# Four tiles of 32 array columns in place of two of 64 for the softmax denominators

## What is computed

```python
h = _layernorm(x, axis=-1) * (1 + ca) + sa
# attention, 8 heads of 64; keys and values come from one latent of 64 columns
q = (h @ Wq.T).reshape(b, t, 8, 64)
kv_latent = h @ Wkv_down.T
k = (kv_latent @ Wk_up.T).reshape(b, t, 8, 64)
v = (kv_latent @ Wv_up.T).reshape(b, t, 8, 64)
scores = jnp.einsum('bqhd,bkhd->bhqk', q, k) * scale
attn = jax.nn.softmax(scores, axis=-1)          # the denominators belong to this
out = jnp.einsum('bhqk,bkhd->bqhd', attn, v)
x = x + ga * (out.reshape(b, t, 512) @ Wo.T)
h = _layernorm(x, axis=-1) * (1 + cb) + sb
x = x + gb * (h @ weight.T + pooled(h) @ disha)
```

## Time and profile before

| | us |
|---|---|
| median of three runs | 3296.38 |
| the profiled execution | 3298.7 |
| its span, first to last instruction | 3296.9 |
| PE busy | 3215.7 (98%) |
| POOL busy | 2569.9 (78%) |
| DVE busy | 2218.1 (67%) |
| ACT busy | 1730.9 (53%) |
| 4096 records of L545 (mixes), busy together | 991.9 |
| 512 records of L631 (denominators), busy together | 133.1 |

### The profile page before, as it was taken

The page is one execution under the profiler, slowest core; times in us unless marked ns, Lnnn a source line. Parts: engine busy times, 40 slices in busy tenths (PEclk is TensorE's granted clock), DMA queues, the critical chain, the costliest instruction groups (busy, mean ns, idle before and its releaser), DMA issues.

```text
span 3296.9 us, 43601 instructions
## 1 busy us (share of the span) xinstructions
PE 3215.7 (98%) x14886; PEld 1944.6 (59%) x14886; DVE 2218.1 (67%) x2542; ACT 1730.9 (53%) x3203; POOL 2569.9 (78%) x1513
## 2 busy tenths in 40 slices
PE   5999999999999999999999999999999999999995
PEld 3555656566566565656566565665666666566554
DVE  4657667776767768667776767768667776766652
ACT  1555555555555555555555555555555555555551
POOL 1778788887887878788887877878788887877882
PEclk7999999999999999999999999999999999999996
DMA  2111120111112011111111112011121111111111
GB/s 67 39 45 53 46 65 33 52 56 46 55 46 65 30 59 52 46 65 33 52 55 46 55 46 65 31 58 52 46 65 33 52 55 46 55 46 52 37 40 35
DMA packets 157644, 163.06 MB, mean 49 GB/s; under 512 B 54384, under 2 KB 105712, under 8 KB 157424
## 3 DMA queue, kind: packets, MB, share of 16 engines
q1 hardware_dynamic: 157424, 160.29, 14.9%
HBM read 74.66 MB, written 17.33 MB: 28 GB/s over the span
## 4 chain that ended last, share of the span: by engine, by line
PE 92%; DVE 5%; POOL 1%; issue 1%; ACT 1%; DMA 1%; SPq 0%; POOLq 0%; ACTq 0%; DVEq 0%
PE ps_mix L545 27%; PE ps_score L563 16%; PE ps_max L584 14%; PE ps_score L565 14%; PE ps_side L533 6%; PE ps_side L644 6%; PE ps_side L631 3%; PE ps_side L662 3%; DVE neg_max L982 1%; DVE w_out_lo L991 1%; PE ps_side L602 1%; POOL prob_sum L840 1%; DVE query L1025 1%; PE ps_side L651 1%; DVE h_lo L1015 1%
## 5 line engine op out<-in xcount | busy, mean ns | idle before, releaser
L840 POOL TENSOR_TENSOR prob_sum<-prob_sum,probs 128x1024 f32<-128x1024 f32 x768 | 1880.9, 2449 | 283.4 <-ACT probs L720 239.3
L982 DVE TENSOR_REDUCE neg_max<-ps_max 128x1 f32<-128x1024 f32 x1024 | 1247.6, 1220 | 776.4 <-PE ps_max L584 769.8
L720 ACT ACTIVATE probs<-ps_score 128x512 f32<-128x512 f32 x2048 | 1114.4, 599 | 945.5 <-PE ps_score L565 921.0
L545 PE MATMUL ps_mix<-probs,values 128*64 128x512 f32 x4096 | 991.9, 605 | 0.0
L563 PE MATMUL ps_score<-query,key_hi 128*128 128x512 f32 x2048 | 874.1, 427 | 1.1 <-ACT probs L720 1.1
L565 PE MATMUL ps_score<-query_m,key_lo 128*128 128x512 f32 x2048 | 807.2, 394 | 0.0
L584 PE MATMUL ps_max<-key_hi,query 128*128 128x512 f32 x2048 | 644.2, 396 | 8.0 <-DVE neg_max L982 5.2
L563 PEld LDWEIGHTS ps_score<-query,key_hi 128*128 128x128 f32 x2048 | 385.6, 188 | 377.1 <-issue 296.9
L545 PEld LDWEIGHTS ps_mix<-probs,values 128*64 128x64 f32 x4096 | 248.7, 136 | 477.3 <-issue 476.5
L840 POOL TENSOR_TENSOR prob_sum<-probs 128x1024 f32<-128x1024 f32 x128 | 320.8, 2507 | 241.1 <-ACT probs L720 241.1
L584 PEld LDWEIGHTS ps_max<-key_hi,query 128*128 128x128 f32 x2048 | 386.9, 190 | 100.9 <-DVE neg_max L982 10.5
(11 more groups left out here) (119 smaller groups left out, 2983.4 us busy)
## 6 DMA issues: line engine op xcount, KB each, us to landing
query_m<-query SPq DMA_DIRECT2D x128, 512.0 KB, 3.2
recip<-recip_scratch SPq DMA_DIRECT2D x256, 128.0 KB, 2.9
x_in<-in_L_attn_x_dram SPq DMA_DIRECT2D x32, 512.0 KB, 4.0
x_mid<-in_L_attn_x_dram SPq DMA_DIRECT2D x64, 256.0 KB, 4.3
out_dram<-x_mid SPq DMA_DIRECT2D x64, 256.0 KB, 2.2
denoms<-recip SPq DMA_DIRECT2D x256, 2.0 KB, 1.8
gates<-gates_scratch SPq DMA_DIRECT2D x16, 256.0 KB, 4.1
query_m<-max_row SPq DMA_DIRECT2D x128, 4.0 KB
```

The source lines that it names most:

```text
L545: last = nc.tensor.matmul(ps_mix[j * R:j * R + R, :], values[par][:, k, :], probs[:, s % RING, j * HALF:(j + 1) * HALF], start=(k == 0), s ...
L720: nc.scalar.activation(probs[:, s % RING, half * HALF:(half + 1) * HALF], ps_score[half], ACT.Exp, scale=SCALE).then_inc(exps_done, 1)
L840: nc.gpsimd.tensor_tensor(out=total[:, :], in0=before, in1=probs[:, s % RING, :], op=ALU.add).then_inc(adds_done, 1)
L982: nc.vector.tensor_reduce(neg_max[:, m:m + 1], ps_max[m % 2][:, :], AX_X, ALU.max, negate=True).then_inc(maxima_done, 1)
```

## The change

The sum over the partitions is taken by four matmuls instead of two. Each has 32 result rows (not 64) and goes over 256 of the 1024 columns (not 512). The result rows q*32 to q*32+31 of `ps_side` then hold the sums of quarter q in columns 0 to 255. The copy by ScalarE is 128 by 256 instead of 128 by 512. The spread to `denoms` takes four DMAs of 32 partitions instead of two of 64, with the same 1024 numbers, and VectorE's wait counts 64 instead of 32 per denominator. Nothing else is touched: the order on every engine is the same, with two more matmuls and two more DMA issues in the places of the old ones.

```diff
+QUARTERS = 4
+QR, QC = P // QUARTERS, T // QUARTERS
 # SP
-for j in range(2):
-    sp.dma_start(denoms[j * R:(j + 1) * R, :], prob_total[j * R:j * R + 1, :]).then_inc(denoms_spread, 16)
+for q in range(QUARTERS):
+    sp.dma_start(denoms[q * QR:(q + 1) * QR, :], prob_total[q * QR:q * QR + 1, 0:QC]).then_inc(denoms_spread, 16)
 # TensorE
-for j in range(2):
-    last = nc.tensor.matmul(side[j * R:(j + 1) * R, :], ones_cols[:, :],
-                            prob_sum[i % 2][:, j * HALF:(j + 1) * HALF], start=True, stop=True)
+for q in range(QUARTERS):
+    last = nc.tensor.matmul(side[q * QR:(q + 1) * QR, 0:QC], ones_cols[:, 0:QR],
+                            prob_sum[i % 2][:, q * QC:(q + 1) * QC], start=True, stop=True)
 # ScalarE
-nc.scalar.activation(prob_total[:, :], ps_side[:, :], ACT.Copy).then_inc(side_drained, 1)
+nc.scalar.activation(prob_total[:, 0:QC], ps_side[:, 0:QC], ACT.Copy).then_inc(side_drained, 1)
 # VectorE
-need(dve, denoms_spread, 32 * (GROUPS * b + i + 1))
+need(dve, denoms_spread, 16 * QUARTERS * (GROUPS * b + i + 1))
```

## The result

The changed kernel took 3261.5 us (median of four runs, 3258.6 to 3262.6), the kernel before 3298.7 (four runs, 3295.1 to 3303.5): a ratio of 0.9889, 95% interval 0.9875 to 0.9904. It is faster by 37 us, 1.1%. Profile against profile the executions took 3262.6 and 3298.7 us, the spans 3260.8 and 3296.9: 36.1 us less either way.

The account below looks back on a forecast made before the run. TensorE's queue, 98% busy, was taken as the bound. Gains of 27.7 and 9.5 us, 37.2 together, less 1.0 and 0.9 gave 35.3: profiled 3298.7 to 3263.4, median forecast 3261 us, range 3247 to 3284.

Parts of the forecast that it names:

- The bound and the share on the path: TensorE's queue bounds the run; denominators hold 3.5% of the chain, 115 us; shorter pieces give 37.2 us.
- The piece behind the mixes: 99 denominators directly behind the mixes on TensorE: 0.86 us each becomes 0.58, 27.7 us gained.
- rivals 1 and 2: Denominator records: 1, only two run at once, 3311 us, chance 0.10; 2, four slow each other, near 3286, chance 0.09.
- The entry: TensorE's switch from 64-column to 32-column tiles before a denominator: 0.13 us taken, bounds 0 and 0.20.
- the rule quoted in the prediction: Trainium skill, array packing: changing the tiling mode drains TensorE, unlike changing the tile; without it 13 us more gained.
- rival 3: The switch into 32-column tiles is hidden altogether: 0.45 us in place of 0.58 for the 99, 3248 us, chance 0.06.
- The piece that waited: 27 denominators that began after a wait on TensorE: 1.08 us each becomes 0.73, 9.5 us gained.
- These waits stay as they are: TensorE's waits ending at denominators keep their length, since VectorE's query, ending the longer, is fed by TensorE and comes earlier.
- ScalarE's copy and SP's issues: Copy 384 ns instead of 598; four DMA issues some 2.3 us instead of 1.14; VectorE keeps 1.5 us of cover.
- rival 4: Slower spread makes VectorE wait for reciprocals and TensorE in part: 32 us given back, about 3293 us, chance 0.05.
- The end: End of the run: 1 us off where POOL is nearly full, 0.9 us lost on the last copy and spread.

Follow-up runs that it names:

- narrow512: Kernel before with only the tile width changed: four tiles of 32 array columns, each still over 512 data columns; 3308.7 us, ratio 1.0033 to the kernel before.
- half64: Kernel before, still two tiles of 64 array columns, each matmul over only the first 256 columns of its half; 3245.7 us, ratio 0.9840.
- thin_add: Changed kernel with two of GpSimd's 56 adds per slot cut to 8 columns and one added to every sum; 3250.9 us, ratio 0.9864 to the kernel before.
- mix4_after: Changed kernel with VectorE's multiplication by the reciprocals one step earlier (MIX_LAG 4 for 5); 3255.8 us, ratio 0.9872 to the kernel before.
- copy512: Changed kernel with ScalarE's copy over all 512 columns as before; 3265.3 us, ratio 0.9894 to the kernel before.
- one_dma: Changed kernel with the spread as one DMA in place of four; 3260.7 us, ratio 0.9885 to the kernel before.
- pair_grouped: Changed kernel's 32-column, 256-data-column matmuls on two tiles only, program order quarters 0, 1, 2, 3; 3311.5 us, ratio 1.0034 to the kernel before.
- pair_turns: Changed kernel's 32-column, 256-data-column matmuls on two tiles only, program order quarters 0, 2, 1, 3; 3305.6 us, ratio 1.0021 to the kernel before.

## Why the prediction was right

The forecast was 3261, the median is 3261.5; the range and the side were right. So close a hit is luck in part: I took 35.3 us off a median of 3296.4; with its fourth run the kernel before has a median of 3298.7, and from there it fell by 37.2. By its steps:

- **The bound and the share on the path.** As said: TensorE is the queue, and the pieces carry the gain. 98 x 0.29 + 27 x 0.44 = 40.3 us on the pieces, where I had 37.2.
- **The piece behind the mixes.** 0.58 forecast, 0.57 measured. Four tiles work together at full rate (rivals 1 and 2 fell; narrow512 and the two pair kernels show that neither the narrow tile nor the short stream makes the gain without it). Against the 3.07 times that the Trainium skill gives for four tiles in rows ("TensorE: Matmul & The Clock Gate", Measured speedup vs the span model), eight records of 0.216, 1.73 us, took 0.45 here behind the entry, 3.8 times.
- **The entry.** 0.13 taken, 0.12 measured, 0.10 of it ahead of the first record; half64, which lacks it, has 0.43 for 0.57. So a change of tiling mode costs something, as the rule quoted in the prediction wants it, and rival 3 fell. That TensorE drains in it no run shows.
- **The piece that waited.** This term was mis-sized: 0.73 forecast, 0.64 measured. I spaced the weight loads 0.03 to 0.04 us apart as with four of them; the eight stand 0.01 apart. It gave 27 x 0.09 = 2.4 us more.
- **"These waits stay as they are".** Wrong: one of two per slot grew from 0.23 to 0.42 us of idle time, 2.5 us in all, since the multiplication now starts while an add of GpSimd runs. thin_add shows the mechanism, mix4_after that the wait is VectorE's. Why the two now meet was not tested by a run; by the rows VectorE comes 0.46 us earlier in relation to GpSimd's adds, from 0.13 behind the end of one to 0.33 ahead of it.
- **ScalarE's copy and SP's issues.** 384 ns and 2.47 us for four issues, near the 384 and 2.3 forecast; VectorE's cover 1.4 us for the 1.5 forecast. Neither matters in mid run (copy512 and one_dma leave the slot as it is), so rival 4 fell.
- **The end.** 1.9 us lost was the forecast: 1.0 for the steps where GpSimd is nearly full, 0.9 for copy and spread. From the first start of the last denominator to the last instruction it took 73.2 us before and takes 74.9 now, 1.7 more. From the copy's start to the multiplication it is 1.1 (8.26 and 9.35 us), near the 0.9. The other 0.6 lies behind it, where the lower clock sets the length of TensorE's pieces (granted clock 0.55 before, 0.51 now) and executions differ by several us. For the steps before, little is missing: see the balance. So this sum was hit in part by luck.

The balance: on the pieces and waits 40.3 - 2.5 = 37.8 us, and from the first denominator to the last it is 3098.3 - 3060.7 = 37.6 us less. With 0.3 us less ahead of the first and 1.7 more behind the last that makes the 36.1 of the spans. Two errors of 2.4 and 2.5 us with opposite signs made the forecast look closer than its terms were.

## What to carry to other kernels

Where TensorE is the bound and a matmul has few result rows, split its data columns over more tiles: here four tiles of 32 array columns in place of two of 64 took 0.45 us in place of 0.86. It pays as long as the streams are long against the switch between tile widths, here 0.12 us in; the 0.20 out to full width was paid before too. Where matmuls of one width stood next to each other the switch was not paid (0.43 from pair to pair), so read its price from the chain before you split. A piece that gets shorter shifts engines against each other: look for operations of VectorE on two SBUF tensors that now meet GpSimd's, and put them into VectorE's idle time, but not so early that VectorE waits for their data: in mix4_after that took the gain back in every third slot.

## What the runs showed of the hardware that was not expected

- VectorE's multiplication of two 128 by 512 float32 tensors takes 0.68 us alone, 0.87 when it meets the end of a GpSimd add, and 1.72 in the mean where most meet one (mix4_after); w_out_lo 0.69 against 2.77. Those that start while an add runs end 0.55 us behind it, and an add that starts just behind a multiplication takes 2.90 us instead of 2.4. The Trainium skill, "GPSIMD Engine Reference", Specifications, says that the SBUF interfaces are shared with VectorE, with contention where an instruction has two SBUF inputs; the runs agree and give the price: the rest of the add, here up to about three times the operation's own length on top of it.
- Matmuls on different tiles overlapped in both orders of the program that were run (pair_grouped and pair_turns, 0.99 us each). That one float32 matmul makes two records is no obstacle: with four tiles four records start within 0.02 us and the other four 0.24 later, with two tiles two and two.
